# Self attention: the negated maxima placed in two score buffers by ScalarE, two banks for all other products, row sums copied out

## The reference, cut to what matters

```python
# x: (8, 512, 256) f32; 16 heads of 64 columns each
def _L1_attn_ref(X, W_qkv, W_out):          # X is the layer norm of x
    ...
    qkv = qkv.reshape(b, s, h, d, 3)
    q, k, v = (qkv[..., 0], qkv[..., 1], qkv[..., 2])
    scores = jnp.einsum('bqhd,bkhd->bhqk', q, k) / scale
    weights = jax.nn.softmax(scores, axis=-1)
    attn = jnp.einsum('bhqk,bkhd->bqhd', weights, v)
    return attn.reshape(b, s, h * d) @ W_out
```

## Time and profile before

| | |
|---|---|
| median of 3 runs | 3022.01 us (3020.82 to 3023.24) |
| the profiled execution | 3020.66 us |
| its span in the profile | 3018.8 us |
| PE (TensorE) busy | 2760.4 us, 91% |
| VectorE (DVE) busy | 1922.6 us, 64% |
| ScalarE (ACT) busy | 1446.6 us, 48% |
| GpSimd (POOL) busy | 1103.7 us, 37% |

### The profile page before, as it was taken

One profiled execution on the slowest core, in us unless ns is written; L12 is line 12 of the kernel. 1 busy time (PEld: TensorE's weight loads), 2 busy tenths in 40 slices (PEclk: granted clock), 3 DMA queues, 4 the chain that ended last, 5 costly groups with the idle time before them and its releaser, 6 DMA issues. The chain is left out here.

```text
span 3018.8 us, 49274 instructions
## 1 busy us (share of the span) xinstructions
PE 2760.4 (91%) x16604; PEld 1622.9 (54%) x16605; DVE 1922.6 (64%) x3109; ACT 1446.6 (48%) x2224; POOL 1103.7 (37%) x853
## 2 busy tenths in 40 slices
PE   7997899999868899999999999999889999966998
PEld 4774333333335555555555555555445555566997
DVE  5775666667668766657575757575645555474565
ACT  2342566666668743434343434343335555543333
POOL 3233332222037243434343434343443333153333
PEclk9998899999979999999999999999989999958999
DMA  5002222222111000000000000000043222146665
GB/s 159 0 0 74 53 58 56 57 57 52 33 56 43 1 1 1 0 0 0 0 0 0 0 0 0 0 0 0 1 110 79 71 67 71 45 113 232 214 218 194
DMA packets 102928, 159.71 MB, mean 53 GB/s; under 512 B 28349, under 2 KB 63432, under 8 KB 97160
## 3 DMA queue, kind: packets, MB, share of 16 engines
q1 hardware_dynamic: 97784, 147.88, 17.0%
q0 software_dynamic: 3408, 8.46, 0.8%
q10 hardware_dynamic: 1600, 1.61, 0.2%
HBM read 91.79 MB, written 14.96 MB: 35 GB/s over the span
## 5 line engine op out<-in xcount | busy, mean ns | idle before, releaser
L1671 DVE TENSOR_REDUCE self_nmax<-self_SM 128x2 f32<-128x1024 f32 x256 | 313.8, 1226 | 185.3 <-PE self_SM L1568 178.5
L522 DVE TENSOR_REDUCE cross_nmax<-cross_S 128x2 f32<-128x1024 f32 x256 | 311.7, 1224 | 153.3 <-PE cross_S L347 152.4
L1709 POOL TENSOR_TENSOR self_U<-self_PT 128x1024 f32<-128x1024 f32 x64 | 153.1, 2392 | 626.0 <-ACT self_PT L1649 626.0
L1649 ACT ACTIVATE self_PT<-self_ST 128x1024 f32<-128x1024 f32 x256 | 262.3, 1025 | 217.1 <-PE self_ST L1591 217.1
L1712 POOL TENSOR_TENSOR self_U<-self_U,self_PT 128x1024 f32<-128x1024 f32 x128 | 304.0, 2375 | 55.2 <-ACT self_PT L1649 50.7
L456 ACT ACTIVATE cross_PT<-cross_S 128x1024 f32<-128x1024 f32 x256 | 260.7, 1025 | 118.0 <-PE cross_S L358 117.1
L1186 DVE TENSOR_REDUCE cross_nmax<-cross_S 128x4 f32<-128x1024 f32 x128 | 156.7, 1224 | 143.3 <-PE cross_S L984 143.1
L1601 PE MATMUL self_OP<-self_PT,self_V 128*64 128x512 f32 x1024 | 233.8, 598 | 10.0 <-ACT self_PT L1649 10.0
L1685 DVE RECIPROCAL self_rcp<-self_W 128x512 f32<-128x512 f32 x64 | 214.1, 3345 | 8.4 <-PE self_W L1608 8.4
L1112 ACT ACTIVATE cross_PT<-cross_S 128x1024 f32<-128x1024 f32 x128 | 131.0, 1023 | 121.4 <-PE cross_S L1000 121.4
L377 PE MATMUL cross_W<-cross_PT,cross_V 128*32 128x512 f32 x1024 | 139.1, 618 | 8.0 <-DVE cross_rsin L554 8.0
(11 more groups left out here) (435 smaller groups left out, 6401.8 us busy)
## 6 DMA issues: line engine op xcount, KB each, us to landing
moe_staged<-in_L_ffn_W SPq DMA_DIRECT2D x36, 1024.0 KB, 5.9
cross_ks<-cross_parts SPq DMA_DIRECT2D x384, 64.0 KB, 2.2
cross_qs<-cross_parts SPq DMA_DIRECT2D x376, 64.0 KB, 2.3
all_x<-in_L_ffn_W SPq DMA_DIRECT2D x14, 1024.0 KB
all_x<-sorted_rows SPq DMA_DIRECT2D x83, 130.0 KB, 2.3
cross_cT<-in_ctx_T SPq DMA_DIRECT2D x16, 512.0 KB, 4.3
sorted_rows<-all_spare_row SPq DMA_DIRECT2D x1, 5460.0 KB, 23.8
all_x<-in_x SPq DMA_DIRECT2D x8, 512.0 KB, 6.1
```

Source lines behind the costliest of these rows:

```text
L522: dve.tensor_reduce(nmax[:, g % 2, 0:R, n % PER_G], S[:, slot[st], :, :], AX.X, ALU.max, negate=True).then_inc(s_maxed, 1)
L1649: act.activation(PT[:, k, :, :], ST[:, :, :], ACT.Exp).then_inc(exped.sem, 1)
L1671: dve.tensor_reduce(nmax[:, i, 0:P:D], SM[:, :, :], AX.X, ALU.max, negate=True).then_inc(maxed.sem, 1)
L1709: pool.tensor_tensor(U[:, c % 2, :, :], PT[:, 0, :, :], PT[:, 1, :, :], ALU.add).then_inc(added.sem, 1)
```

## The change

ST becomes two buffers of two banks. OP goes, and the ring W shrinks from three banks to two, which now also carry `av` (8 banks: ST 4, SM 2, W 2). The fourth pair of every exact step goes. In its place `mt` becomes two ring steps, one for each head: PE transposes the column of maxima broadcast to 128 columns, so that each partition of the result holds the whole row of maxima, and ScalarE copies it to `least`. Then ScalarE copies `least` into both ST buffers (two 128x1024 copies), and after the exponentials of k0 and k1 it copies it again into the buffer just read. The exact products then add onto what ScalarE has put there (no product of the three starts a new sum). The second `mt` step stands behind the v or norm step. The row sums are copied to SBUF by ScalarE, and VectorE takes the reciprocal there, in place. Four small products at the start of the stage set ST up for adding. Two fills on GpSimd in the feed-forward stage go (128x128 and 128x512).

```diff
-                    add("mt", c + 1, NC)
+                    add("mt", (c + 1) * 2, NC * 2)
                     if c < NT:
                         add("v", NT + c, HALF * NT)
                     if c == 5:
                         add("norm", KC + 1, KC)
                     if c >= 6:
                         add("v", HALF * NT + 2 * (c - 6), HALF * NT)
+                    add("mt", (c + 1) * 2 + 1, NC * 2)
...
-    RINGED = ("q", "k", "v", "norm", "mt", "sum", "out")
+    RINGED = ("q", "k", "v", "norm", "mt", "av", "sum", "out")
...
-        return "act" if kind in ("v", "mt") else "dve"
+        return "act" if kind in ("v", "mt", "av", "sum") else "dve"
...
-    BANKS = 3
+    BANKS = 2
...
-        ST = s.ps("ST", [P, 2, 512])
+        ST = s.ps("ST", [P, 2, 2, 512])
         SM = s.ps("SM", [P, 2, 512])
-        OP = s.ps("OP", [P, 512])
...
                 elif kind == "mt":
+                    c, j = n // 2, n % 2
                     dst = free_bank(pe, b, order, st)
-                    reach(pe, maxed, "max", b, order, ("max", n * NT + NT - 1, rel))
+                    if j == 0:
+                        reach(pe, maxed, "max", b, order, ("max", c * NT + NT - 1, rel))
                     for i in range(NT):
-                        m = pe.transpose(dst[:, i * P:(i + 1) * P], nmax[:, i, :], ident)
+                        m = pe.transpose(dst[:, i * P:(i + 1) * P], nmax[:, i, j:j + 1].to_broadcast([P, P]), ident)
...
-                    exped.wait(pe, b, n_exact)
-                    n_exact += 1
+                    filled.wait(pe, b, n - 1)
...
-                            pe.matmul(ST[:, j, :], l[at, slot, at_k], r[at, slot, :], start=(t == 0), stop=False)
-                    for j in range(2):
-                        at = slice(j * D, (j + 1) * D)
-                        m = pe.matmul(ST[:, j, :], ones_r[at, :], mrow[at, :], start=False, stop=True)
+                            m = pe.matmul(ST[:, n % 2, j, :], l[at, slot, at_k], r[at, slot, :], start=False, stop=(t == 2),
+                                          skip_group_check=True)
...
                     exped.wait(pe, b, NT * (n + 1))
-                    lifted.wait(pe, b, n)
+                    dst = free_bank(pe, b, order, st)
...
# ScalarE
                 elif kind == "mt":
-                    act.copy(mrow[:, :], src).then_inc(drained["act"].sem, 1)
+                    c, j = n // 2, n % 2
+                    done_before = 0 if order is first else NT * (NC if rel else c)
+                    if j == 0:
+                        filled.wait(act, b, done_before and done_before - 2)
+                    act.copy(least[:, j, :], src).then_inc(drained["act"].sem, 1)
+                    if j == 1:
+                        drained["act"].wait(act, b, order.nth["act"][st])
+                        for k in range(2):
+                            exped.wait(act, b, done_before and done_before - 1 + k)
+                            act.copy(ST[:, k, :, :], least[:, :, :]).then_inc(filled.sem, 1)
+                elif kind == "sum":
+                    scaled.wait(act, b, n)
+                    act.copy(rcp[:, :], src).then_inc(drained["act"].sem, 1)
...
-                    act.activation(PT[:, k, :, :], ST[:, :, :], ACT.Exp).then_inc(exped.sem, 1)
+                    act.activation(PT[:, k, :, :], ST[:, n % 2, :, :], ACT.Exp).then_inc(exped.sem, 1)
+                    if k < 2:
+                        exped.wait(act, b, n + 1)
+                        act.copy(ST[:, n % 2, :, :], least[:, :, :]).then_inc(filled.sem, 1)
...
# VectorE
                 elif kind == "sum":
-                    ring_full.wait(dve, b, order.nth["ring"][st])
-                    scaled.wait(dve, b, n)
-                    dve.reciprocal(rcp[:, :], bank_of(order, st)).then_inc(done, 1)
-                    drained["dve"].wait(dve, b, order.nth["dve"][st])
-                    lifted.wait(dve, b, n + 1)
+                    drained["act"].wait(dve, b, order.nth["act"][st])
+                    dve.reciprocal(rcp[:, :], rcp[:, :]).then_inc(inverted.sem, 1)
+                    inverted.wait(dve, b, n + 1)
                     dve.tensor_tensor(OT[:, n, :], Oraw[:, n % 2, :], rcp[:, :], ALU.mult).then_inc(scaled.sem, 1)
```

More of the change, by code:

```diff
@@ L1374, in __init__ @@
         self.hT_hi, self.hT_lo = s.sb("hT_hi", [P, KC, T], F32R), s.sb("hT_lo", [P, KC, T], F32R)
-        self.nmax, self.ones_r, self.ones = s.sb("nmax", [P, NT, P]), s.sb("ones_r", [P, P], F32R), s.sb("ones", [P, 64])
+        self.nmax, self.ones = s.sb("nmax", [P, NT, 2]), s.sb("ones", [P, 64])
         self.half, self.eps, self.minus = (s.sb(n, [P, NT]) for n in ("half", "eps", "minus"))
@@ L1448, in self_attention @@
                "split": lambda kind: kind in ("q", "k", "norm")}
-    for kind in ("exact", "max", "av", "sum"):
+    for kind in ("exact", "max", "sum"):
         counted[kind] = lambda k, kind=kind: k == kind
@@ L1498, in self_attention @@
         guarded, maxed = loop("guarded", "max"), loop("maxed", "max")
-        valued, lifted = loop("valued", "av"), loop("lifted", "av")
-        scaled = loop("scaled", "sum")
+        scaled, inverted = loop("scaled", "sum"), loop("inverted", "sum")
+        filled = Loop(s.sem("filled"), NC * NT, 2)
         added = Loop(s.sem("added"), 3 * NC)
@@ L1621, in scalar_steps @@
                 kind, n, rel = st
-                if kind in RINGED and kind not in ("sum", "out"):
+                if kind in RINGED and kind != "out":
                     ring_full.wait(act, b, order.nth["ring"][st])
@@ L1648, in scalar_steps @@
                     added.wait(act, b, 3 * (c - 1) + max(k, 1))
-                    act.activation(PT[:, k, :, :], ST[:, :, :], ACT.Exp).then_inc(exped.sem, 1)
+                    act.activation(PT[:, k, :, :], ST[:, n % 2, :, :], ACT.Exp).then_inc(exped.sem, 1)
+                    if k < 2:
+                        exped.wait(act, b, n + 1)
+                        act.copy(ST[:, n % 2, :, :], least[:, :, :]).then_inc(filled.sem, 1)
                 elif kind == "av":
-                    valued.wait(act, b, n + 1)
                     scaled.wait(act, b, n - 1)
-                    act.copy(Oraw[:, n % 2, :], OP[:, :]).then_inc(lifted.sem, 1)
+                    act.copy(Oraw[:, n % 2, :], src).then_inc(drained["act"].sem, 1)
         def vector_steps(dve, b, order):
@@ L1670, in vector_steps @@
                     guarded.wait(dve, b, n_max)
-                    dve.tensor_reduce(nmax[:, i, 0:P:D], SM[:, :, :], AX.X, ALU.max, negate=True).then_inc(maxed.sem, 1)
+                    dve.tensor_reduce(nmax[:, i, :], SM[:, :, :], AX.X, ALU.max, negate=True).then_inc(maxed.sem, 1)
                 elif kind in ("q", "k", "norm"):
@@ L1716, in _ @@
             def _(pe):
+                for k in range(2):
+                    for j in range(2):
+                        pe.matmul(ST[:, k, j, :], wq[:, 0, 0:P], hT_hi[:, 0, :], start=True, stop=True)
                 tensor_steps(pe, None, first)
-                for counter in (ring_full, scored, guarded, valued):
+                for counter in (ring_full, scored, guarded):
                     counter.credit(pe)
@@ L1726, in _ @@
                 scalar_steps(act, None, first)
-                for counter in (drained["act"], split, exped, lifted, normed):
+                for counter in (drained["act"], split, exped, filled, normed):
                     counter.credit(act)
@@ L1735, in _ @@
                 vector_steps(dve, None, first)
-                for counter in (drained["dve"], s_stat, maxed, scaled):
+                for counter in (drained["dve"], s_stat, maxed, scaled, inverted):
                     counter.credit(dve)
```

13 lines of the change are left out of this document (5 added, 8 removed).

## The result

The changed kernel takes a median of 3063.23 us (3057.25 to 3073.23, four runs) against 3021.41 (3019.29 to 3023.24) for the kernel before beside it: a ratio of 1.0142, 95% interval 1.0114 to 1.017, or 41.8 us more. Forecast were 3057, which is 35 more, and a range of 3036 to 3082. The profiled execution took 3063.43 us, its span is 3061.6.

A forecast was written before the change was run, and what follows sets the result against it. PE was taken as the bound. A batch costs +4.9 us, seven 34.4; the last gains about 1.0 and the start costs 1.5: +34.9 on 3020.66 is 3055.6, with the median 1.35 higher 3057, range 3036 to 3082.

The forecast's parts named there:

- The gain: Exact products on PE: 0.23 us a removed pair, three of four counting in an ordinary round, 0.69.
- The second `mt` step: Ring on PE: `av` must wait until v's bank is drained, 1.11 us after the last v product instead of 0.33: +0.78.
- Rounds 1, 2 and 6: Ordinary rounds: three removed pairs against the later `av`, −0.69 + 0.78 = +0.09 us each.
- Rival 1: Copies keep up and PE keeps what it was given: 3009 us, or 2996 with the pair of k0 counted; chance 0.12.
- Rival 3: A draw, the banks costing half of what was counted: 3022 to 3028 us; chance 0.05.
- Round 0: ScalarE late through the exponential's table load; first transposes 0.6 us earlier, `av` 0.78 later: +0.2.
- round 3: `htok` stands ahead of the sums' copy on ScalarE, and v waits for that bank: +0.50 + 0.78 = +1.3 us.
- round 4: Nothing between `mt` and `av`; `av` waits for the copy of the first maxima, 0.49 us more: −0.2 in all.
- round 5: `av` takes the second norm step's bank, drained by VectorE's low half behind reciprocal and multiplication: +2.9 us.
- round 7: The pair of k0 counts too, −0.92 + 0.78, and the last `out` product's factor comes 0.6 us later: +0.45.
- The fills: ScalarE's 1024-column fills: 1.03 us each, 0.89 to 1.2 possible, covered in ordinary rounds; ScalarE about 75% of a round.
- Rival 2: VectorE bounds through its port shared with GpSimd; the reciprocal in SBUF waits for GpSimd's additions: 3107 us; chance 0.07.

The follow-up runs named there:

- e1: The kernel before without its fourth pair; maxima still found and transposed but not subtracted: 2975.21 us, ratio 0.9843.
- e3: The changed kernel without the second transposes; ScalarE copies the first head's maxima for the second head, fills and copies as many: 2987.81 us, ratio 0.9883.
- e9: The changed kernel with all eight transposes of maxima put into SM, no `mt` step in the ring, `htok` in round 4: 2998.53 us, ratio 0.9922.
- e2: The kernel before with `av` in a ring of two banks and the sums copied by ScalarE; pair and single `mt` kept: 3032.12 us, ratio 1.0035.
- e4: The changed kernel with the second norm step moved right behind the first, before the sums: 3039.22 us, ratio 1.0051.
- e5: The changed kernel with `htok` moved from k2 of round 3 to the end of round 4's k3: 3055.71 us, ratio 1.0116.
- e6: The changed kernel with each fill writing 4 columns instead of 1024, maxima hardly subtracted, all waits kept: 3038.07 us, ratio 1.005.
- e8: The changed kernel with norm steps together, `htok` in round 4, and sums, q, k, v and inversion reordered within the round: 3058.33 us, ratio 1.0121.
- e12: The kernel before with one wait a batch added: `av` of round 5 waits for VectorE's low half of the second norm step: 3060.69 us, ratio 1.0117.
- e10: The changed kernel with one maximum for both heads, so one `mt` step, and `htok` in round 4: 2980.39 us, ratio 0.9859.
- e7: The changed kernel with both norm steps together before the sums and `htok` in round 4: 3035.76 us, ratio 1.0044.
- e11: The changed kernel without ScalarE's copy of the sums; VectorE takes the reciprocal straight from PSUM: 3269.85 us, ratio 1.0813.

## Why the prediction was right, and where it fell short

**The gain** was 0.23 a pair, three of four: e1 shows 0.70 and 47 us in all.

**The second `mt` step** was called +0.78 by way of V's bank, with `av` at 1.11 after v. It is 1.06, and e3 and e9 take it away from two sides (75 and 65 us, the latter with `htok`'s 8 in it). e9 keeps all the transposes and is 10.7 over e3, or 18 without the gain from `htok`. So of the 75 some 18 are the transposes themselves and some 57 the place in the ring with the clock behind it (an estimate from these medians). Rounds 1, 2 and 6 came at −0.04 for +0.09, the other way than forecast. Rival 1, PE keeping what it was given, did not come in the changed kernel; e9 comes nearest to it, with −0.31 in an ordinary round where that rival had −0.17. Rival 3, the draw, did not come either: the two banks alone cost 10 (e2), and what they were made to carry cost the rest.

**Special rounds.** Round 0 +0.03 for +0.2, round 3 +1.15 for +1.3, round 4 −0.45 for −0.2, round 5 +2.91 for +2.9, round 7 +0.21 for +0.45. Every sign of these is right; together the batch is 3.7 for 4.9, and e2, e4 and e5 show the named causes of rounds 3 and 5 one by one.

**The fills** took 1.013 and 1.017 for 1.03, and ScalarE is 76% busy in round 1 for about 75%. That they are hidden in ordinary rounds is e6's result, and so is their 1.3 in round 0. The Trainium skill ("ScalarE: Activation LUTs", Step-by-step: what each stage is for) has PSUM as the lower-latency port of this engine. The runs agree, by an amount that changes nothing: of 512 columns copied to SBUF, a source in SBUF takes 0.624 (e3) where PSUM takes 0.587, but of 1024 columns the copy from SBUF to PSUM takes 1.013 to 1.017 and the one from PSUM to SBUF 1.015 (e9), so writing PSUM saves about 0.04 (an estimate from these).

**Rival 2**, the port shared with GpSimd, is refuted: the reciprocal in SBUF takes 3.349 for 3.345 from PSUM, and starts as soon as the sums are there while GpSimd is adding. The Trainium skill ("SBUF — State Buffer", Who interferes with whom) does not have it on its list, and these 4 ns agree. The multiplication even became shorter, 1.163 for 1.670; in round 5 it starts 0.43 before the end of GpSimd's third addition, where it started 0.88 before it, and ends as long after that end as before.

**The step that failed** is the sum over batches: "A batch: 0.2 + 3 × 0.09 + 1.3 − 0.2 + 2.9 + 0.45 = 4.9. Seven batches 34.4". It takes all seven as alike and prices a wait of PE at its length. The batch was overstated by 1.2, 8 in all: 0.13 to 0.25 in every round but round 5. In round 1 the wait of `av` was 0.05 shorter than forecast, and the rest is there without that wait: e3 is 0.77 under the kernel before where the pair was put at 0.69. Left out was that behind the waits of rounds 5 and 0 the granted clock drops to 1.2 GHz in three batches, 13 in all. With 3.4 for 1.5 at the start of the stage, 0.7 for 1.0 in the last batch and 0.8 outside the stage this leaves 42.8 against 34.9 forecast. That the two large errors partly cancel is luck, and the range held because it was made wide for other reasons.

**What stays open.** Why the same wait, at the same place, with the same instructions ahead of it, is followed by 1.2 GHz in one batch and not in the next. Why the feed-forward ahead of the stage ends up to 5.0 us earlier (e5, e8) and 4.7 later (e12) than in the kernel before, although the experiments do not touch it and the change itself only took two small fills on GpSimd from it. And, with one profiled execution of each kernel, how much of the difference in the number of such stretches is the kernel's and how much the execution's: the four executions of the changed kernel alone lie between 3057 and 3073.

## What to carry to other kernels

In a ring of banks look at each step's wait for the step exactly as many places earlier as there are banks, and at how fast that one is drained: adding one short step (0.42 us of transposes) moved a consumer onto the bank filled last, and cost 75 us, some 18 of them its own, while shrinking the ring by itself cost 10. Before giving a new product a place in a tight ring, look for a buffer that is idle at that moment, as SM was in e9. And where PE is the bound and runs at its full clock, price a wait of one to four us at its length, and add for a part of its occurrences what a drop of the clock costs behind it, 1.3 to 3.0 here.

## What the runs showed that was not expected

- **Short waits and the clock.** PE is busy for over 90% of the stage, and a single idle stretch of 1.29 us (round 0) or 2.53 us (round 5) is followed by 3 to 7 us at 1.2 GHz in three batches of seven, at a cost of 1.35 and 2.95. With a wait of 3.82 (e12) it is six of seven.
- **The length of the wait alone does not decide.** The wait of 1.26 to 1.29 us ahead of round 0's first transposes stands in eight of the kernels here. It is followed by the lower level in none of seven batches in e3, in one in e4 and e10, two in e9, three in e7, five in e5 and all seven in e11. In e11 waits of 2.4 us in rounds 3 and 6 are followed by it in none of the seven full batches.
- **Which wait is followed by it differs between kernels that are alike there.** With `htok` in round 4 (e5) it is round 5 of every batch; with thin fills (e6) it is two. Two such kernels differ by some 10 us for that alone. That the edits did this is not shown.
- **A broadcast source costs nothing.** Eight transposes of one column read as 128 take 0.84 us in e9, where four of a full tile took 0.42.
- **The fill of a score buffer**, ScalarE's copy from SBUF into PSUM, takes 1.017 us for 1024 columns and 0.165 for 4 (e6): 0.84 ns a column.
